# Another cyclic order for the first layer, and the second layer's first buffers loaded while the experts run

## The chip, the cores and the metric

One core of a Trainium2 chip runs one program. Its engines are TensorE (matmuls and transposes), VectorE, ScalarE, GpSimd and SyncE, whose queue issues most DMAs. The metric is the device time of one execution in microseconds. The kernel before takes 4163.48 us, the median of three runs from 4163.27 to 4163.56.

## The reference, cut to what matters

`x` is (64, 128, 256), the context (64, 128, 192), everything float32. Two layers follow each other, each an attention over the context and then a feed-forward part:

```python
x = x + xattn0(layernorm(x), ctx_768, mask)   # 16 heads of 16, masked keys
x = x + moe(layernorm(x))                     # switch router over 8 experts, capacity 512
x = x + xattn1(layernorm(x), ctx_768)         # 16 heads, then relu(out @ W1 + b1) @ W2 + b2
x = x + cells(layernorm(x))                   # 6 nodes, each an 8-head self-attention
```

The router counts, over all tokens in order, how many went to each expert; token 513 and later of an expert keep their input. A cell node forms q, k and v from three edges `We` out of earlier nodes, scaled by `ew`, then applies `Wq`, `Wk`, `Wv`. The kernel multiplies each edge with its projection beforehand ("fusing", pieces F and B), which is eighteen 256 x 256 products.

## The kernel before, in words

Three blocks follow each other; each begins when every engine has ended the one before.

**First layer** (`phase_first_layer`). The 64 sequences are 32 jobs of two. Each engine runs through a written list. A table such as `FIRST_PE_ORDER` is one period; `name:s` means that in period k the piece is done for job k - s (`unfold`). So different jobs are interleaved, and an engine never leaves its list's order. The pieces on TensorE are: `Tx` transposes the normed rows, `Q`, `K`, `V` project, `S0` and `S1` are the scores of either sequence, `T0.0` to `T1.1` transpose the probabilities (two strips each), `A` is attention times V, `O` the output projection, `Tn` transposes the second norm's rows, `L` makes router logits, and `r.n` ranks tokens within experts for each group of four jobs. VectorE takes the strips' maxima (`x`), reciprocals (`i`), copies out of PSUM (names with `^`), statistics (`st`, `st1`) and the routing steps `r.sh`, `r.oh`. ScalarE does the exponentials (`e`) and the copies of transposed probabilities (`T..^`). GpSimd scales the probabilities (`n`), norms rows (`rs`, `nm`, `rs1`, `nm1`) and scatters routed rows with indirect DMAs (`put`).

SyncE's list is written out (`load`, `store`). The context buffer `ct` has two halves. `load(j)` (L282) fetches x and then the context:

```python
                if j >= 2:
                    sp.wait_ge(prod, max(n_prod["K", j - 2], n_prod["V", j - 2]))
                sp.dma_start(ct[:, j % 2], halves(ctx[j])).then_inc(c_in[j % 2], 16)
```

and `K` and `V` of job j wait for `c_in`. `store(j)` (L291) waits for `x1_made` and for `nm1` of job j. The last lines of SyncE's list are stores 29 and 30, then the loads for fusing pieces 3, 4 and 5 (each waits for `B` three before, L280 and L279), then store 31. `FUSE_PE_PLACES` and `FUSE_DVE_PLACES` say behind which piece of which job (counted from the last) a fusing piece is inserted.

**Experts** (`phase_experts`). Eight experts in turn, each 512 rows: transpose, 256 to 1024 with relu, 1024 to 256. SyncE loads rows, w1 and w2 of expert e when expert e - 2 has freed its buffer, and unfused cell weights.

**Second layer** (`phase_second_layer`). Again 32 jobs and one table per engine. `f.` pieces are the cross attention, S, T, A, Q, K, V, O with a digit are a cell node, `e.` the end. Twelve fusing pieces (F6 to F17) are inserted into the first periods; their four buffers lie in `probs` and `probsT`. `f.ga` on GpSimd gathers expert outputs into `routed` with an indirect DMA, `f.x2` on VectorE adds them to x, `f.st`, `f.rs` and `f.x` norm the result, `f.Tx` transposes it. At the end `e.f1` and `e.f2` on GpSimd form the single buffer `fin`, and `e.f1(j)` waits for the store of job j - 1. SyncE's loop is:

```python
            for j in range(2, JOBS):
                load_rows(j)      # waits for f.Tx(j-1)
                load_context(j)   # waits for f.K and f.V of j-1
                if j >= JOBS_IN_FLIGHT:
                    store(j - JOBS_IN_FLIGHT)
```

with `JOBS_IN_FLIGHT` 3; `store` waits for `fin_made`.

Of the kernel before, what the change touches and what calls it, by code (L numbers as in the profile page):

```python
# [139 lines left out]
def phase_first_layer(nc, io, scratch, keep, cst, consts_in, cell, w1_first):  # L140
# [794 lines left out]
def phase_second_layer(nc, io, scratch, keep, cell, cst, out):  # L935
# [52 lines left out]
    def rows(ap, j):  # L988
        return ap.rearrange("(g b) t d -> g t b d", b=PAIR)[j]

    with ExitStack() as es:
# [6 lines left out]
        wq, wk, wv = (sb(n, [2, D]) for n in ("wq", "wk", "wv"))
        w1, w2 = sb("w1", [2, HID * P]), sb("w2", [HID, D])
        bq, bk, bv, b1 = sb("bq", [2]), sb("bk", [2]), sb("bv", [2]), sb("b1", [HID])  # L1000
        b2, ln_g, ln_b = sb("b2", [D]), sb("ln_g", [D]), sb("ln_b", [D])
        x2, x3 = sb("x2", [JOBS_IN_FLIGHT, PAIR, D]), sb("x3", [JOBS_IN_FLIGHT, PAIR, D])
        xg, xn, x5, fin = sb("routed", [PAIR, D]), sb("xn", [PAIR, D]), sb("x5", [PAIR, D]), sb("fin", [PAIR, D])
        ct, xT, qF, kE, kO = (sb(n, [2, W2]) for n in ("ctxT", "xT", "front_qT", "front_kT_even", "front_kT_odd"))
        oF = xT
# [12 lines left out]
        late = [(t[:, 2 * h].rearrange("p j t -> p (j t)").rearrange("p (c n) -> p c n", n=D),  # L1018
                 t[:, 2 * h + 1].rearrange("p j t -> p (j t)").rearrange("p (c n) -> p c n", n=D))
                for t in (pr[:, 1], pT[:, 1]) for h in range(2)]  # L1020
# [40 lines left out]
        def halves(a):  # L1061
            return a.rearrange("(c p) n -> p c n", p=P)

        def late_load(eng, n):
            c, k, edge = fused[n]
            weT, we = late[n % LATE_RING]
            eng.dma_start(weT, halves(io["edgesT"][edge])).then_inc(late_in[n % LATE_RING], 16)
            eng.dma_start(we, halves(io[("L1_ffn_Wq", "L1_ffn_Wk", "L1_ffn_Wv")[k]][c])).then_inc(late_in[n % LATE_RING], 16)
# [4 lines left out]
        def _(sp):  # L1073
            def store(j):
                sp.wait_ge(fin_made, j + 1)
                sp.dma_start(rows(out, j), fin[:]).then_inc(stored[j % 2], 16)
# [8 lines left out]

            def load_context(j):
                if j >= 1:
                    sp.wait_ge(prod, max(n_prod["f.K", j - 1], n_prod["f.V", j - 1]))
                sp.dma_start(ct[:], halves(ctx[j])).then_inc(c_in[j % 2], 16)

            def fuse_load(n):
                sp.wait_ge(prod, n_prod[f"B{n - LATE_RING}", 0])
                late_load(sp, n)
# [490 lines left out]
```

## Time and profile before

| | us |
|---|---|
| median of the runs | 4163.48 |
| the profiled execution | 4160.97 |
| its span, first to last instruction | 4159.2 |
| TensorE busy in the span | 4031.4 (97%) |
| ScalarE busy | 2628.5 (63%) |
| VectorE busy | 2472.9 (59%) |
| GpSimd busy | 1932.9 (46%) |
| mean granted TensorE clock | 0.99 |

The first layer fills the first 653 us or so, the experts 657 to 896, the second layer the rest. In rows of the timeline the first number is the start in us, the second the duration, then engine, line and operation, what it writes and reads, how many instructions are merged, and in brackets how long the engine sat idle just before and what ended that. L12 is line 12 of the kernel. A landing time counts from the issue of a DMA to its completion.

### The profile page before, as it was taken

The page shows a single profiled execution, that of the slowest core. Times are in us where ns is not written, and L with a number is a line of the kernel's source. Part 1 is how long each engine was busy: PE and PEld are TensorE (multiplying, and loading weights), DVE is VectorE, ACT ScalarE, POOL GpSimd, SP SyncE. Part 2 cuts the span into 40 slices and gives each one's busy share as a digit, 9 for nine tenths or more (in the row PEclk, how much of TensorE's full clock was granted, in tenths as well). Part 3 has the DMA queues.
Part 4 walks back from the last instruction along what each step waited for, and adds up shares of the span by engine and source line. Part 5 has one row for each costly group of instructions (what it writes and reads, how often), then busy time and mean ns, then how long its engine had stood idle before and what let it go on. Part 6 is the DMA issues. An engine that isn't in the chain of part 4 may idle for free.

```text
span 4159.2 us, 100757 instructions
## 1 busy us (share of the span) xinstructions
PE 4031.4 (97%) x38276; PEld 3405.7 (82%) x38276; DVE 2472.9 (59%) x6184; ACT 2628.5 (63%) x11786; POOL 1932.9 (46%) x2011
## 2 busy tenths in 40 slices
PE   7999998988999999999999999999999999999997
PEld 6888876666888888888888888888888888888885
DVE  5777772024566666666666666666666666666553
ACT  6888871214666666666666666666666666666664
POOL 6888982113444444444444444444444444444332
PEclk9999999999999999999999999999999999999999
DMA  3232214430000000000000000000000000000000
GB/s 102 70 98 72 70 45 140 132 116 23 12 14 14 14 17 21 13 14 14 13 13 16 13 13 13 12 12 12 12 12 12 12 20 12 12 12 12 7 4 6
DMA packets 117867, 129.75 MB, mean 31 GB/s; under 512 B 12006, under 2 KB 110676, under 8 KB 117264
## 3 DMA queue, kind: packets, MB, share of 16 engines
q1 hardware_dynamic: 101664, 106.26, 8.0%
q0 software_dynamic: 6144, 8.43, 0.7%
q10 hardware_dynamic: 9584, 8.61, 0.7%
q8 instruction: 312, 5.11, 0.5%
q14 instruction: 163, 1.34, 0.1%
HBM read 89.68 MB, written 41.94 MB: 32 GB/s over the span
## 4 chain that ended last, share of the span: by engine, by line
PE 75%; DVE 1%; ACT 1%; DMA 0%; POOL 0%; issue 0%; ACTq 0%; POOLq 0%; SPq 0%; DVEq 0%
PE c_product L1374 35%; PE c_product L1385 15%; PE c_product L1433 10%; PE c_scores L1423 7%; PE c_product L1456 5%; PE c_product L1444 2%; ACT c_probs L1187 1%; DVE c_qT L1233 1%; PE c_product L1362 1%; PE c_product L1493 0%; DVE c_neg_max L1242 0%; DMA c_probsT<-in_L_ffn_Wk 0%; ACT c_front_probs L1187 0%; POOL c_probs L1135 0%; DMA c_probsT<-in_L_ffn_Wv 0%
## 5 line engine op out<-in xcount | busy, mean ns | idle before, releaser
L1135 POOL TENSOR_TENSOR c_probs<-c_probs,c_row_inv 128x512 f32<-128x512 f32 x768 | 794.2, 1044 | 1525.8 <-DVE c_row_inv L1245 1525.1
L1187 ACT ACTIVATE c_probs<-c_scores,c_neg_max 128x128 f32<-128x128 f32 x3072 | 1086.6, 409 | 606.1 <-DVE c_neg_max L1242 606.1
L1374 PE MATMUL c_product<-c_nodes,cell_w 128*128 128x256 f32 x4352 | 1064.2, 384 | 6.1 <-DVE c_nodes L1233 3.9
L1374 PEld LDWEIGHTS c_product<-c_nodes,cell_w 128*128 128x128 f32 x4352 | 802.6, 190 | 133.1 <-DVE c_nodes L1233 12.8
L1187 ACT ACTIVATION_READ_ACCUMULATOR c_probs<-c_scores,c_neg_max 128x1 f32 x3072 | 762.1, 248 | 0.0
L1242 DVE TENSOR_REDUCE c_neg_max<-c_scores 128x4 f32<-128x512 f32 x1024 | 635.6, 683 | 179.7 <-PE c_scores L1423 179.5
L1193 ACT COPY c_probsT<-c_product 128x512 f32<-128x512 f32 x768 | 416.2, 611 | 237.8 <-PE c_product L1433 235.0
L1187 ACT ACTIVATE c_front_probs<-c_scores,c_neg_max 128x128 f32<-128x128 f32 x1024 | 359.0, 401 | 149.0 <-DVE c_neg_max L1242 149.0
L1385 PE MATMUL c_product<-cell_w,c_nodes 128*128 128x256 f32 x1792 | 432.7, 381 | 1.6 <-DVE c_kT L1233 1.6
L1433 PE MATMUL c_product<-consts_sb,c_probs 128*128 128x128 f32 x3072 | 403.1, 275 | 15.2 <-POOL c_probs L1135 15.0
L420 ACT ACTIVATE a_probs<-a_scores,a_neg_max 128x128 f32<-128x128 f32 x1024 | 361.9, 399 | 82.3 <-DVE a_neg_max L476 81.7
L1433 PEld LDWEIGHTS c_product<-consts_sb,c_probs 128*128 128x128 f32 x3072 | 349.7, 141 | 59.5 <-POOL c_probs L1135 21.2
L1385 PEld LDWEIGHTS c_product<-cell_w,c_nodes 128*128 128x128 f32 x1792 | 332.8, 190 | 47.7 <-DVE c_kT L1233 1.9
L1135 POOL TENSOR_TENSOR c_front_probs<-c_front_probs,c_row_inv 128x512 f32<-128x512 f32 x256 | 266.7, 1057 | 179.7 <-DVE c_row_inv L1245 179.6
L1374 PE MATMUL c_product<-c_oT,cell_w 128*128 128x256 f32 x1280 | 328.7, 379 | 1.3 <-DVE c_oT L1233 1.3
L1245 DVE RECIPROCAL c_row_inv<-c_row_sum 128x4 f32<-128x4 f32 x1024 | 171.7, 168 | 183.8 <-ACT c_probs L1187 140.8
L1233 DVE TENSOR_SCALAR c_nodes<-c_product,cell_b 128x256 f32<-128x256 f32 x320 | 140.0, 479 | 236.8 <-PE c_product L1374 236.8
L1233 DVE TENSOR_SCALAR c_qT<-c_product,cell_b 128x256 f32<-128x256 f32 x384 | 167.8, 478 | 180.6 <-PE c_product L1374 180.6
L1374 PEld LDWEIGHTS c_product<-c_oT,cell_w 128*128 128x128 f32 x1280 | 243.0, 190 | 35.0 <-DVE c_oT L1233 2.0
L369 POOL TENSOR_TENSOR a_probs<-a_probs,a_row_inv 128x512 f32<-128x512 f32 x256 | 259.3, 1047 | 26.6 <-DVE a_row_inv L479 26.6
L1233 DVE TENSOR_SCALAR c_oT<-c_product,cell_b 128x256 f32<-128x256 f32 x384 | 168.1, 479 | 159.3 <-PE c_product L1456 156.8
L1187 ACT ACTIVATION_READ_ACCUMULATOR c_front_probs<-c_scores,c_neg_max 128x1 f32 x1024 | 246.3, 240 | 0.0
(167 smaller groups left out, 6679.4 us busy)
## 6 DMA issues: line engine op xcount, KB each, us to landing
e_w<-in_L_ffn_w SPq DMA_DIRECT2D x12, 1024.0 KB, 6.5
a_x<-in_x SPq DMA_DIRECT2D x32, 256.0 KB, 2.9
a_ctxT<-in_ctx_pairsT SPq DMA_DIRECT2D x32, 256.0 KB, 3.1
x<-a_x SPq DMA_DIRECT2D x32, 256.0 KB, 2.2
xn<-a_xn SPq DMA_DIRECT2D x32, 256.0 KB, 2.1
c_routed<-xn SPq DMA_DIRECT2D x32, 256.0 KB, 2.9
c_x<-x SPq DMA_DIRECT2D x32, 256.0 KB, 3.2
c_ctxT<-in_ctx_pairsT SPq DMA_DIRECT2D x32, 256.0 KB, 2.8
```

Of the source, the lines that this page charges most:

```text
L369: nc.gpsimd.tensor_tensor(p, p, rinv[:, j % 2, b, r].unsqueeze(2).broadcast_to([P, 4, T]), ALU.mult).then_inc(norm_made, 1)
L420: a = nc.scalar.activation(pr[:, j % 2, b, r, k], S[r][:, k], ACT.Exp, bias=nmax[:, j % 2, b, r, k:k + 1], accum_out=rsum[:, j % 2, b, r, ...
L1135: nc.gpsimd.tensor_tensor(e, e, rinv[:, i, r].unsqueeze(2).broadcast_to([P, 4, T]), ALU.mult).then_inc(norm_made, 1)
L1187: a = nc.scalar.activation(probs(n)[:, r, k], S[r][:, k], ACT.Exp, bias=nmax[:, i, r, k:k + 1], accum_out=rsum[:, i, r, k:k + 1])
L1193: nc.scalar.copy(probsT(n)[:, int(n[-1])], bank(n, j)[:]).then_inc(pT_made, 1)
L1233: k = V.tensor_scalar(dst[:, u], m[:, u], bias[:, u:u + 1], scalar, ALU.add, *([then] if then else []))
L1242: V.tensor_reduce(nmax[:, i, r], S[r][:], AX.X, ALU.max, negate=True).then_inc(max_made, 1)
L1374: i = T_.matmul(m[:, u], w[:, k, u * P:(u + 1) * P], src[:, k], start=n == 0, stop=n == last)
L1385: i = T_.matmul(m[:, b], src[:, k, b * T:(b + 1) * T], w[:, k], start=n == 0, stop=n == len(steps) - 1)
L1423: i = T_.matmul(S[r][:, k], q[e, u, b * T:(b + 1) * T], w[e, u, b * T:(b + 1) * T], start=True, stop=True)
L1433: i = T_.transpose(m[:, k], probs(name)[:, r, k], ident)
L1456: i = T_.matmul(m[32 * r:32 * r + 32, u, b * T:(b + 1) * T], va[:, group(c), b, h:h + 32], pT[:, group(c), r, k], start=True, stop=True)
```

## The change

The tables of the first layer are replaced, and with them the places of its fusing pieces; the ring of `xn1` has seven places instead of six. The second layer's weights, biases, the buffers of its first four fusing pieces and the rows, x and context of its job 0 are allocated before the experts and loaded by SyncE in their loop; the engines' own loads at the start of the second layer are gone. The first expert's w1 now lies in `front_probs`. The first w2 waits for the first rows. In the second layer, `front_oT` gets a buffer of its own, two memsets move behind the first gather, and the store moves.

```diff
 FIRST_PE_ORDER = """
-K:1 T0.1:3 S1:2 Tx:1 A:3 r.n:6 Q:1 O:3 T1.0:2 T0.0:2 S0:1 V:1 L:5 Tn:4 T1.1:2
+S1:2 A:3 Tx:1 Tn:6 O:3 r.n:7 Q:1 T0.0:2 S0:1 V:2 T0.1:2 K:0 L:6 T1.0:2 T1.1:2
 FIRST_DVE_ORDER = """
-r.oh:5 S0.i0:1 K^:0 S0.i1:1 S1.x0:1 Tx^:0 S1.x1:1 S1.x3:1 S1.i0:1 A^:2 r.n^:5 S1.x2:1 S1.i1:1 Q^:0 S1.i3:1
-O^:2 S0.i3:1 S1.i2:1 st1:2 S0.i2:1 S0.x0:0 S0.x1:0 S0.x3:0 V^:0 L^:4 r.sh:4 mk:-1 st:-1 S0.x2:0 Tn^:3
+r.oh:6 S1.x3:1 S0.i2:1 S1.x2:1 A^:2 S1.x1:1 Tx^:0 S1.x0:1 Tn^:5 r.n^:6 S1.i3:1 O^:2 Q^:0 S1.i1:1 S1.i0:1
+S1.i2:1 S0.x1:0 S0.x3:0 S0.x0:0 S0.x2:0 V^:1 mk:-1 st:-1 K^:-1 L^:5 r.sh:5 st1:2 S0.i1:0 S0.i3:0 S0.i0:0
 FIRST_ACT_ORDER = """
-S1.e1:1 S1.e3:1 S1.e2:1 T1^0:1 T1^1:1 T0^0:1 T0^1:1 S0.e0:0 S0.e1:0 S0.e3:0 r.ex:4 T1^2:1 S0.e2:0 T1^3:1
-T0^3:1 T0^2:1 S1.e0:0
+T1^0:5 T1^3:5 T1^2:5 S1.e3:4 S1.e2:4 S1.e1:4 S1.e0:4 T0^0:4 T0^1:4 S0.e1:3 S0.e0:3 T0^2:4 T0^3:4 S0.e3:3
+S0.e2:3 r.ex:8 T1^1:4
 FIRST_POOL_ORDER = """
-rs:1 nm:1 rs1:4 S0.n0:2 nm1:4 S0.n1:2 S1.n0:2 S1.n1:2 S1.n3:2 S1.n2:2 S0.n3:2 S0.n2:2 put:9
+S0.n1:3 S0.n2:3 nm1:5 S1.n3:3 S1.n1:3 S1.n0:3 S1.n2:3 put:11 rs:1 nm:1 rs1:4 S0.n3:2 S0.n0:2
 FUSE_PE_PLACES = """
-Tn:1 F0
-L:1 B0
-Tn:0 F1
-L:0 B1 F2 F3
-r.n:0 B2 B3 F4 F5 B4 B5
+L:5 F0
+T1.0:1 B0 F1
+Tn:4 B1
+L:4 F2
+T1.0:0 B2 F3
+T1.1:0 B3 F4
+Tn:3 B4
+L:3 F5
+Tn:2 B5
...
-    X_RING, ROW_RING, GROUP = 4, 6, 4
+    X_RING, ROW_RING, GROUP = 4, 7, 4
... phase_experts, SyncE
+            sp.wait_ge(rows_in[0], 16)
             sp.dma_start(w2t[:, 0], tiles(w2[0])).then_inc(w2_in[0], 16)
...
+                if e == 4:
+                    for n, a in (("wk", "L1_xattn_Wk_rows"), ("wq", "L1_xattn_Wq"), ("wv", "L1_xattn_Wv_rows"),
+                                 ("w1", "L1_xattn_W1"), ("w2", "L1_xattn_W2")):
+                        sp.dma_start(early[n][:], tiles(io[a])).then_inc(early[n + "_in"], 16)
+                if e == 5:
+                    for n in ("bq", "bk", "bv", "b1"):
+                        sp.dma_start(early[n][:], io[f"L1_xattn_{n}_cols"]).then_inc(early["column_biases_in"], 16)
+                    for n, a in (("b2", "L1_xattn_b2"), ("ln_g", "L1_ffn_ln_g"), ("ln_b", "L1_ffn_ln_b")):
+                        sp.dma_start(early[n][:], io[a].partition_broadcast(P)).then_inc(early["row_biases_in"], 16)
+                if e == 6:
+                    for n in range(FUSED_FIRST, FUSED_FIRST + len(early["late"])):
+                        fuse_load(sp, io, fused, n, early)
+                if e == E - 1:
+                    sp.dma_start(early["routed"][:], rows_of(scratch["xn1"], 0)).then_inc(early["rows0_in"], 16)
+                    sp.dma_start(early["x"][:, 0], rows_of(scratch["x1"], 0)).then_inc(early["x0_in"], 16)
+                    sp.dma_start(early["ctxT"][:], tiles(io["ctx_pairsT"][0])).then_inc(early["ctx0_in"], 16)
... phase_second_layer, SyncE
-FRONT_NODES, JOBS_IN_FLIGHT = 2, 3
+FRONT_NODES, JOBS_IN_FLIGHT, STORES_BEHIND = 2, 3, 5
...
             for j in range(2, JOBS):
                 load_rows(j)
+                if j >= STORES_BEHIND:
+                    store(j - STORES_BEHIND)
                 load_context(j)
-                if j >= JOBS_IN_FLIGHT:
-                    store(j - JOBS_IN_FLIGHT)
-            for j in range(JOBS - JOBS_IN_FLIGHT, JOBS):
+            for j in range(JOBS - STORES_BEHIND, JOBS):
                 store(j)
```

`phase_first_layer`'s SyncE list and its context buffer are not edited.

## Rows read from the trace of the kernel before

**Rows 1.** Busy time by stage; columns are window, length, then each engine's us
```profile
100.00:600.00 500.00, 479.42 (x5845) 413.61 (x5844) 382.24 (x1064) 417.28 (x1941) 444.62 (x478) 0.99 0.23 72
660.00:896.00 236.00, 230.99 (x832) 154.06 (x832) 21.46 (x32) 43.98 (x64) 21.19 (x19) 0.98 0.36 120
1200.00:4000.00 2800.00, 2797.34 (x26917) 2401.20 (x26917) 1750.03 (x4260) 1855.71 (x8369) 1214.36 (x1246) 1.00 0.04 13
```
**Rows 2.** Timeline of VectorE, the copy of oT, one per job, eight jobs apart
```profile
122.79 0.69 DVE L501 COPY a_oT<-a_product 128x512 f32<-128x512 f32 x1
270.99 0.69 DVE L501 COPY a_oT<-a_product 128x512 f32<-128x512 f32 x1
```
**Rows 3.** Windows of 10 us with idle of TensorE; the clock stands third from the end
```profile
150.00:160.00 10.00, 7.43 (x111) 6.29 (x114) 9.28 (x33) 6.67 (x32) 6.63 (x9) 1.00 0.00 1
...
300.00:310.00 10.00, 7.32 (x112) 6.20 (x114) 9.16 (x32) 6.57 (x32) 8.33 (x10) 0.87 0.07 23
...
530.00:540.00 10.00, 8.22 (x89) 7.13 (x90) 7.82 (x25) 5.81 (x32) 7.71 (x9) 0.83 0.24 79
```
**Rows 4.** Timeline near the start: V of job 1, a turn, the context load
```profile
41.12 1.99 PE L618 MATMUL a_product<-a_wv,a_ctxT 128*128 128x256 f32 x8
42.95 1.04 PE L651 MATMUL a_product<-consts_sb,a_probs 128*128 128x128 f32 x8
43.15 0.37 SPq L289 DMA_DIRECT2D a_ctxT<-in_ctx_pairsT  x1
```
**Rows 5.** Landing times in us: of L289 in the first layer, and second layer medians
```profile
DMA to landing us min/median/max: 2.5/3.1/8.3
...
out<-c_fin SPq DMA_DIRECT2D x28, 256.0 KB, 2.2
...
c_ctxT<-in_ctx_pairsT SPq DMA_DIRECT2D x27, 256.0 KB, 2.8
c_routed<-y,slots POOLq DMA_INDIRECT x54, 2.7
```
**Rows 6.** Timeline of TensorE, a turn and the K behind it
```profile
150.61 1.04 PE L651 MATMUL a_product<-consts_sb,a_probs 128*128 128x128 f32 x8
151.49 1.89 PE L611 MATMUL a_product<-a_ctxT,a_wk 128*128 128x256 f32 x8
```
**Rows 7.** Timeline of the first layer's tail, each engine
```profile
595.17 0.39 PE L632 MATMUL a_scores<-a_mask_add,a_one_row 32*128 32x512 bf16 x4
...
619.47 1.94 PE L662 MATMUL a_product<-a_probsT,a_v_even_odd 128*32 128x128 f32 x60 [0.82 <-ACT a_probsT L426]
...
621.04 2.43 POOL L355 TENSOR_SCALAR a_xn<-a_x,a_mean_var,a_rstd 128x256 f32<-128x256 f32 x2 [0.30 <-DMA buf<-a_xn,slots]
...
649.85 0.98 POOL L396 DMA_INDIRECT buf<-a_xn,slots  x1 [0.30 <-issue]
...
657.74 0.36 SPq L761 DMA_DIRECT2D e_rows<-buf  x1
```
**Rows 8.** Timeline of the second layer's start
```profile
896.97 0.37 SPq L1081 DMA_DIRECT2D c_routed<-xn  x1
...
903.95 3.78 PE L1374 MATMUL c_product<-c_probsT 128*128 128x256 f32 x8 [10.35 <-DMA c_probsT<-in_L_ffn_Wq]
...
908.86 1.99 PE L1374 MATMUL c_product<-c_probsT 128*128 128x256 f32 x8
...
918.55 0.60 PE L1362 MATMUL c_product<-consts_sb,c_routed 128*128 128x128 f32 x4
```
**Rows 9.** Timeline of one period of the second layer
```profile
2047.03 1.28 POOL L1162 TENSOR_TENSOR c_fin<-c_x,c_ln_g 128x512 f32<-128x512 f32 x1 [0.23 <-DVE c_x L1227]
...
2048.17 0.60 PE L1362 MATMUL c_product<-consts_sb,c_routed 128*128 128x128 f32 x4
...
2053.31 1.08 POOL L1141 DMA_INDIRECT c_routed<-y,slots  x1 [1.70 <-DMA c_routed<-xn]
...
2059.38 1.63 DVE L1252 SCALAR_TENSOR_TENSOR c_x<-c_routed,gates,c_x 128x256 f32<-128x256 f32 x2
...
2063.91 1.04 PE L1433 MATMUL c_product<-consts_sb,c_probs 128*128 128x128 f32 x8
```

More of the change, by code:

```diff
@@ L55, with rows_of, half_rows, fuse_load @@
 TO_Q, TO_K, TO_V, EDGE, OUT = range(KINDS)
+def rows_of(ap, j):
+    return ap.rearrange("(g b) t d -> g t b d", b=PAIR)[j]
+def half_rows(a):
+    return a.rearrange("(c p) n -> p c n", p=P)
+def fuse_load(eng, io, fused, n, early):
+    c, k, edge = fused[n]
+    r = n % len(early["late"])
+    weT, we = early["late"][r]
+    eng.dma_start(weT, half_rows(io["edgesT"][edge])).then_inc(early["late_in"][r], 16)
+    eng.dma_start(we, half_rows(io[("L1_ffn_Wq", "L1_ffn_Wk", "L1_ffn_Wv")[k]][c])).then_inc(early["late_in"][r], 16)
 def cell_plan():
@@ L729, in phase_experts @@
     plan = cell_plan()
+    fused = fused_weights(plan)
     with ExitStack() as es:
@@ L932, with phase_second_layer @@
 """
-def phase_second_layer(nc, io, scratch, keep, cell, cst, out):
+def phase_second_layer(nc, io, scratch, keep, cell, cst, early, out):
     ctx = io["ctx_pairsT"]
@@ L996, in sem @@
             return es.enter_context(nc.semaphore("c_" + name))
[L998 to L1005, printed above, removed]
+        wq, wk, wv, w1, w2 = (early[n] for n in ("wq", "wk", "wv", "w1", "w2"))
+        bq, bk, bv, b1, b2, ln_g, ln_b = (early[n] for n in ("bq", "bk", "bv", "b1", "b2", "ln_g", "ln_b"))
+        xg, x2, ct, pr, pT, prF = (early[n] for n in ("routed", "x", "ctxT", "probs", "probsT", "front_probs"))
+        x3 = sb("x3", [JOBS_IN_FLIGHT, PAIR, D])
+        xn, x5, fin = sb("xn", [PAIR, D]), sb("x5", [PAIR, D]), sb("fin", [PAIR, D])
+        xT, qF, kE, kO = (sb(n, [2, W2]) for n in ("xT", "front_qT", "front_kT_even", "front_kT_odd"))
+        oF = sb("front_oT", [2, W2])
         vE, vO = sb("v_even", [PAIR, D]), sb("v_odd", [PAIR, D])
@@ L1059, in bank, with loaded @@
             return M[bank_of[n, j] % BANKS]
[L1061 to L1068, printed above, removed]
+        def loaded(eng, pair, first, j):
+            eng.wait_ge(*((first, 16) if j == 0 else (pair[j % len(pair)], 16 * ((j - 1) // len(pair) + 1))))
         block = es.enter_context(nc.Block())
@@ L1075, in store, with next_fuse_load @@
                 sp.wait_ge(fin_made, j + 1)
-                sp.dma_start(rows(out, j), fin[:]).then_inc(stored[j % 2], 16)
+                sp.dma_start(rows_of(out, j), fin[:]).then_inc(stored[j % 2], 16)
             def load_rows(j):
-                if j >= 1:
-                    sp.wait_ge(prod, n_prod["f.Tx", j - 1])
-                sp.dma_start(xg[:], rows(scratch["xn1"], j)).then_inc(r_in[j % 2], 16)
+                sp.wait_ge(prod, n_prod["f.Tx", j - 1])
+                sp.dma_start(xg[:], rows_of(scratch["xn1"], j)).then_inc(r_in[j % 2], 16)
                 if j >= JOBS_IN_FLIGHT:
                     sp.wait_ge(x3_done, j - JOBS_IN_FLIGHT + 1)
-                sp.dma_start(x2[:, j % JOBS_IN_FLIGHT], rows(scratch["x1"], j)).then_inc(x_in[j % JOBS_IN_FLIGHT], 16)
+                sp.dma_start(x2[:, j % JOBS_IN_FLIGHT], rows_of(scratch["x1"], j)).then_inc(x_in[j % JOBS_IN_FLIGHT], 16)
             def load_context(j):
[L1087 to L1093, printed above, removed]
-            load_rows(0)
-            load_context(0)
-            for t, a, got in ((wk, "L1_xattn_Wk_rows", wk_in), (wq, "L1_xattn_Wq", wq_in), (wv, "L1_xattn_Wv_rows", wv_in)):
-                sp.dma_start(t[:], halves(io[a])).then_inc(got, 16)
-            fuse_load(FUSED_FIRST + LATE_RING)
+                sp.wait_ge(prod, max(n_prod["f.K", j - 1], n_prod["f.V", j - 1]))
+                sp.dma_start(ct[:], half_rows(ctx[j])).then_inc(c_in[j % 2], 16)
+            def next_fuse_load(n):
+                sp.wait_ge(prod, n_prod[f"B{n - len(late)}", 0])
+                fuse_load(sp, io, fused, n, early)
+            later = list(range(FUSED_FIRST + len(late), len(fused)))
+            next_fuse_load(later[0])
             load_rows(1)
-            for n in range(FUSED_FIRST + LATE_RING + 1, len(fused)):
-                fuse_load(n)
+            for n in later[1:]:
+                next_fuse_load(n)
             load_context(1)
@@ L1137, in _ @@
                 elif n == "f.ga":
-                    pool.wait_ge(r_in[j % 2], 16 * (j // 2 + 1))
+                    loaded(pool, r_in, early["rows0_in"], j)
                     for b in range(PAIR):
```

81 lines of the change are left out of this document (42 added, 39 removed).

## The prediction

> **What bounds the kernel now.** I read the stage windows first. In the first layer (100 to 600 us) TensorE is busy 479.42 of 500 us, GpSimd 444.62 and ScalarE 417.28; in the second layer (1200 to 4000) TensorE is busy 2797.34 of 2800 [rows 1]. So the second layer has nothing to give on TensorE and can only lose, the first layer has 4.1% of idle, and the rest lies at the seams: 600 to 660, and the start of the second layer.
>
> Then the rhythm of the first layer, from VectorE's copies of `oT`, one per job: eight jobs take 270.99 - 122.79 = 148.2 us, 18.53 each [rows 2]. With 95.9% busy that is 17.77 us of TensorE work per job and 0.76 of idle. The idle sits in the job of each group of four that carries the routing: 7.43 of 10 us busy at 150, 7.32 at 300, the last at 530 [rows 3].
>
> Then the DMA queue: which event lets a context load go, and how long it takes to land [rows 4, 5]. This decides the case.
>
> **The change part by part.**
>
> *First layer, context loads (the largest term).* `ct` has two halves. SyncE may issue the load for job j only when K(j-2) and V(j-2) are done, and K(j) on TensorE waits for it. The old table has V:1 and K:1: V(j-2) is in period j-1 and K(j) in period j+1, with more than a period between. The new table reads `V:2 T0.1:2 K:0`: unfolded, V(j-2), T0.1(j-2), K(j). Only one turn stands between the instruction that frees the buffer and the one that needs it full. The ring and the wait are not edited. In the trace V(1) starts at 41.12 and ends at 43.11, and SyncE issues the context load at 43.15 [rows 4]. That transfer lands in 2.5 at least and 3.1 at the median, behind another load; the same transfer of the second layer, which leaves alone as this one now will, takes 2.8 [rows 5]. So K could start at 43.15 + 2.8 + 0.1 = 46.05. TensorE would be ready earlier: the turn begins at 42.95 [rows 4] and holds it 151.49 - 150.61 = 0.88 [rows 6], to 43.83. The wait is 2.2 us (1.9 with 2.5, 2.5 with 3.1). TensorE issues in order, and behind K(j) stand L, T1.0, T1.1, S1, A and the rest of its period, so nothing fills it. The period becomes 17.77 + 2.2 = 19.97 if every other wait goes, 1.44 more than now. The first jobs sit in the fill, where TensorE is idle for other reasons; 28 jobs remain: 28 x 1.44 = **+40** (32 to 49). The gain that the new order brings, 0.76 per job or 21 us in all, is already taken in full here.
>
> *The clock after such waits.* The granted clock fell in some of the old idle stretches and not in others: 1.00 at 150 to 160, 0.87 at 300 to 310, 0.83 at 530 to 540 [rows 3]; of six such stretches three fell. One fall costs 0.13 to 0.17 of 10 us. New waits are of similar length but in one piece. I take one in four: 7 x 1.5 = **+10**; ends 0 and, if all fall, 28 x 1.5 = 42.
>
> *First layer, tail.* Old: from S0(31) at 595.17 the last A ends at 619.47 + 1.94 = 621.41 (26.2 later), the last scatter is issued at 649.85, and the experts' first load leaves at 657.74 [rows 7]. New: F3 and F4 stand before A(31). But F3's weights are loaded by SyncE behind store(30), which waits for nm1(30): GpSimd ended that at 621.04 + 2.43 = 623.47, 28.3 after S0(31) [rows 7]. Two stores' and loads' issue (0.9) and a landing of 3.1 [rows 5] put F3 at 32.3. TensorE's own work from S0(31) to F3 is about 25 (seven projections of 1.83, six turns of 0.88, and small pieces, by the strides in [rows 4, 6]), so it waits some 7 us; with F3, T1.1, B3, F4 and A another 7, A(31) ends near 39.5, 13.3 later than now. V(30) and one turn, 2.7 us, have moved behind S0(31), which leaves 10.6. Behind A(31) the chain O, `nm1`, Tn, L, routing, scatter is unchanged, but the fusing pieces no longer hold up its TensorE steps; I give 3 back: **+8** (from -3, if that chain turns out shorter by all that the pieces took, to +12).
>
> *Experts.* Twenty-three small loads go into SyncE's stream. Each expert's loads are issued an expert or more ahead of their use and TensorE is busy 230.99 of 236 us [rows 1]; they are hidden, 0. Holding the first w2 back until the rows are in may bring 0.5 at the start: **-0.5** (-1 to +1). If the cover is gone, one late weight load costs its landing, some 3 us [rows 5].
>
> *Start of the second layer.* Old: its first issue is at 896.97, TensorE starts F6 at 903.95 after 10.35 of idle for the fused weights, F7 waits again until 908.86, and f.Tx starts at 918.55 [rows 8]. New: all four buffers are there. F7 to F10 with their pieces take 918.55 - 908.86 = 9.7, F6 and B6 2.6 more: f.Tx at 896.97 + 12.3 = 909.3, 9.2 earlier. GpSimd's gather can leave at 896.97 and its landing, statistics and normalising fit in those 12 us. What is late next is F11's load, issued only after f.Tx as before, so all behind it shifts as a block: **-9** (-6 to -11; low clock at the start may keep 2).
>
> *Second layer, the store's place.* Store(j-5) is now issued in iteration j, just behind load_rows(j), which waits for f.Tx(j-1). e.f1(j-4) of that same period needs that store landed, since `fin` is one buffer. Old: e.f1 ran at 2047.03, before f.Tx (2048.17) had even ended [rows 9]. New: f.Tx ends at 2048.77, two loads are issued, the store leaves near 2049.7 and lands 2.2 later alone [rows 5], up to 1 more behind the loads: e.f1 starts near 2052.7, 5.7 late. Behind it on GpSimd stand e.f2, S3.n0 and the gather. The gather used to wait for its rows until 2053.31 [rows 9]; now it starts near 2056.4, its second half near 2057.8, and lands 2.7 later [rows 5], at 2060.5 to 2061.2. VectorE's f.x2 started at 2059.38 [rows 9], so it is 1.1 to 1.9 late, and behind it O0^ ends near 2063.7. TensorE needs O0^'s bank for T3.1, which began at 2063.91 [rows 9]. So the whole delay just fits: 27 periods at 0.1, **+2** (0 to 27 x 0.7 = 19). Nothing is gained by the move, TensorE being full.
>
> *Own buffer for `front_oT`, memsets behind the gather, seven rings for xn1*: off the path, 0 (-1 to +1).
>
> Sum: 40 + 10 + 8 - 0.5 - 9 + 2 = +50.5 on the profiled execution's 4160.97, whose span is 4159.2. The runs' median is 2.5 higher: about **4213**.
>
> **The rivals.**
> 1. *The clock falls at every context wait.* For: half the old stretches fell, with no longer idle. Against: the other half didn't. 4213 - 10 + 42 = 4245. The Trainium skill ("TensorE: Matmul & The Clock Gate", section "HAM oscillation") tells of a kernel that alternates short bursts with DMA waits and drops to the low clock in every one; the trace only half agrees.
> 2. *The store in the second layer bites.* If the store lands a microsecond later than I think, T3.1 waits 0.6 in 27 periods: 4213 + 14 = 4227.
> 3. *Faster: the context is not late.* It decides if K(j) finds its context landed, by a load issued earlier than V(j-2)'s end. Then the period is 17.8: 28 x -0.7 = -20, tail +8, start -9, second layer +2: 4144. Against it stand the rows of the issue, 0.04 after V's end.
> 4. *The wait is smaller*: landing 2.5, no clock loss, a tail no worse than before: 32 - 9 + 2 puts it near 4189.
>
> **How the numbers follow.** Forecast 0.60 (its own range 4195 to 4235), rival 1 0.17, rival 2 0.10, rival 3 0.06, rival 4 0.07. The range 4185 to 4250 takes in all but rival 3 and the ends. A measurement tells 0.2% (8 us) from no change; faster is rival 3 alone, 0.06; the same 0.02; slower 0.92.
>
> **What would show it.** TensorE idle about 2.2 us before each L611 matmul that reads `ctxT`, put down to the DMA of `ctxT`, about thirty times; `oT` copies 20 us apart, all alike; a wait of several us before an `edge_w` matmul near the end of the layer; F6 within a microsecond of the block's start; GpSimd's `c_fin` waiting for the DMA of `out`. No wait on `ctxT`, or a period under 18.5, would refute me.

## The result, and the profile after

The changed kernel takes 4309.71 us (median of 4 runs, 4300.49 to 4322.68) beside 4163.52 for the kernel before (4163.27 to 4163.81): ratio 1.0355, 95% interval [1.0342, 1.0368]. It is slower, as forecast, but by 146 us and not by 50. The profiled execution of after has a span of 4311.1 us and a mean clock of 0.975.

Split at marks that both traces have ([rows 7, 8] for before), the spans differ like this:

| stretch | before | after | more | forecast |
|---|---|---|---|---|
| start to the mask matmul of S0(31) | 595.17 | 688.97 | +93.8 | +47 (40 + 10, less the 2.7 moved behind) |
| S0(31) to the end of A(31) | 26.24 | 41.90 | +15.7 | +13.3 |
| A(31) to the experts' first load | 36.33 | 38.81 | +2.5 | -3 |
| that load to f.Tx of job 0 | 260.81 | 254.65 | -6.2 | -9.5 |
| f.Tx to the end | 3240.65 | 3286.77 | +46.1 | +2 |

Windows of after, in the columns of [rows 1]: window, length, each engine's us, then clock, DMA share and GB/s.

```profile
100.00:600.00 500.00, 434.48 (x4944) 379.12 (x4943) 325.66 (x906) 356.89 (x1660) 376.76 (x403) 0.92 0.21 64
...
1300.00:4100.00 2800.00, 2761.77 (x26442) 2363.98 (x26441) 1766.87 (x4194) 1823.43 (x8234) 1188.27 (x1228) 1.00 0.04 13
```

In the first layer TensorE is idle for 65 of 500 us where it was idle for 21, and the clock is 0.92 where it was 0.99 [rows 1]: two losses, idle and slow work. In the second layer the window reads a clock of 1.00 as before, and 38 us of 2800 are idle, where 2.7 were. The waits of TensorE in the first layer (total, times, longest):

```profile
PE a_product L636 <- DMA a_ctxT<-in_ctx_pairsT: 63.8, 30, 2.9
PE a_product L643 <- DVE a_oT L526: 21.3, 9, 3.9
```

The first row is the predicted wait: 30 times 2.1 us. The second was not foreseen. The rhythm shows the whole effect on the steady part. VectorE's copies of `oT` for jobs 4 and 28, first in before (its job 4 is the first row of [rows 2]), then in after:

```profile
571.66 0.69 DVE L501 COPY a_oT<-a_product 128x512 f32<-128x512 f32 x1
```

```profile
133.35 0.69 DVE L526 COPY a_oT<-a_product 128x512 f32<-128x512 f32 x1 [0.44 <-PE a_product L687]
...
664.42 0.69 DVE L526 COPY a_oT<-a_product 128x512 f32<-128x512 f32 x1 [0.44 <-PE a_product L687]
```

Over these 24 jobs one takes 18.70 us in before and 22.13 in after: 3.43 more, where the prediction had 1.44 more and a period of 19.97. TensorE's timeline around both waits (start, duration, instruction; in brackets the idle before it and what ended it):

```profile
200.60 3.59 PE L643 MATMUL a_product<-a_wo,a_oT 128*128 128x256 f32 x8 [3.74 <-DVE a_oT L526]
...
213.34 3.06 PE L636 MATMUL a_product<-a_ctxT,a_wk 128*128 128x256 f32 x8 [2.03 <-DMA a_ctxT<-in_ctx_pairsT]
216.19 1.72 PE L643 MATMUL a_product<-a_wsw,a_xn1T 128*128 128x8 f32 x8
217.75 3.49 PE L676 MATMUL a_product<-consts_sb,a_probs 128*128 128x128 f32 x16
...
235.78 1.99 PE L636 MATMUL a_product<-a_ctxT,a_wk 128*128 128x256 f32 x8 [2.01 <-DMA a_ctxT<-in_ctx_pairsT]
237.61 0.95 PE L643 MATMUL a_product<-a_wsw,a_xn1T 128*128 128x8 f32 x8
238.42 2.01 PE L676 MATMUL a_product<-consts_sb,a_probs 128*128 128x128 f32 x16
...
255.72 3.78 PE L636 MATMUL a_product<-a_ctxT,a_wk 128*128 128x256 f32 x8 [2.76 <-DMA a_ctxT<-in_ctx_pairsT]
```

Read the durations: K takes 1.99 us behind one wait and 3.06 or 3.78 behind another; the same L takes 0.95 or 1.72, the same pair of turns 2.01 or 3.49. After some waits the engine runs its next matmuls at the lower of its two levels (1.2 GHz), after others of the same length it doesn't. By windows of 10 us the granted clock is 0.71 at 210, 0.75 at 250 and 0.78 at 560, and 1.00 at 160. The Trainium skill ("TensorE: Matmul & The Clock Gate", section "HAM oscillation") has the clock fall in every DMA wait of a loop whose bursts of 2 us alternate with waits of 3 to 5 us. The waits here are shorter and lie about 20 us apart, and only a part of them is followed by the low clock: the trace agrees in part.

The tail of after, SyncE's and TensorE's rows; they answer to [rows 7]:

```profile
716.83 0.36 SPq L322 DMA_DIRECT2D xn<-a_xn  x1
717.24 0.47 SPq L304 DMA_DIRECT2D a_edgeT<-in_edgesT  x1
717.75 0.51 SPq L305 DMA_DIRECT2D a_edge_w<-in_L_ffn_Wq  x1
...
769.68 0.36 SPq L787 DMA_DIRECT2D e_rows<-buf  x1
```

```profile
688.97 0.39 PE L657 MATMUL a_scores<-a_mask_add,a_one_row 32*128 32x512 bf16 x4
...
720.99 3.78 PE L636 MATMUL a_product<-a_edge_w,a_edgeT 128*128 128x256 f32 x8 [6.87 <-DMA a_edge_w<-in_L_ffn_Wq]
...
728.92 1.95 PE L687 MATMUL a_product<-a_probsT,a_v_even_odd 128*32 128x128 f32 x64
```

F3 waits 6.87 us for weights that SyncE issues right behind store(30): as forecast (7). F3 begins 32.0 after S0(31) (forecast 32.3), A(31) ends 41.9 after it (39.5).

The start of the second layer, against [rows 8]:

```profile
1008.71 3.06 PE L1390 MATMUL c_product<-c_probsT 128*128 128x256 f32 x8 [3.42 <-PEq L757]
...
1013.12 3.51 PE L1390 MATMUL c_product<-c_probsT 128*128 128x256 f32 x8
...
1017.28 1.97 PE L1390 MATMUL c_product<-c_probs 128*128 128x256 f32 x8
...
1024.33 0.60 PE L1378 MATMUL c_product<-consts_sb,c_routed 128*128 128x128 f32 x4
```

The 10.35 us of idle are gone. F6 and F7 take 3.06 and 3.51 us where F8 takes 1.97, after 3.42 us of idle at the block's border, so about 3 of the 9 us are lost again to slow work: 6 stay.

The second layer's waits, all engines and TensorE's (columns as above); before had no such row on `c_fin` for a DMA:

```profile
POOL c_fin L1186 <- DMA out<-c_fin: 179.3, 27, 8.5
DVE c_x L1264 <- DMA c_routed<-y,slots: 47.3, 27, 3.8
PE c_product L1449 <- DVE c_nodes L1245: 33.6, 27, 2.3
```

One period of it, to be laid on [rows 9], whose f.Tx began at 2048.17 (here 2174.18):

```profile
2174.18 0.60 PE L1378 MATMUL c_product<-consts_sb,c_routed 128*128 128x128 f32 x4
...
2175.73 0.47 SPq L1104 DMA_DIRECT2D out<-c_fin  x1
...
2179.03 1.27 POOL L1186 TENSOR_TENSOR c_fin<-c_x,c_ln_g 128x512 f32<-128x512 f32 x1 [6.21 <-DMA out<-c_fin]
...
2182.80 1.08 POOL L1162 DMA_INDIRECT c_routed<-y,slots  x1 [0.17 <-issue]
...
2185.24 3.03 POOL L1156 TENSOR_TENSOR c_probs<-c_probs,c_row_inv 128x512 f32<-128x512 f32 x3
...
2187.03 2.92 DVE L1264 SCALAR_TENSOR_TENSOR c_x<-c_routed,gates,c_x 128x256 f32<-128x256 f32 x2 [1.55 <-DMA c_routed<-y,slots]
...
2191.01 1.06 PE L1449 MATMUL c_product<-consts_sb,c_probs 128*128 128x128 f32 x8 [0.92 <-DVE c_nodes L1245]
```

Counted from f.Tx: e.f1 at 4.85 (forecast 4.5), the gather at 8.6 (8.2), f.x2 at 12.9 (before 11.2, forecast 12.3 to 13.1). So far all as worked out. Then f.x2 takes 2.92 us, not 1.63, and T3.1 begins at 16.8 where it began at 15.7: 1.1 us late in this period, not 0.1. The step has come to lie beside four products of GpSimd on end, the three above and

```profile
2188.23 1.03 POOL L1156 TENSOR_TENSOR c_front_probs<-c_front_probs,c_row_inv 128x512 f32<-128x512 f32 x1
```

where in before one of 1.19 us lay beside it. The 27 periods from job 4 on, in before and in after, columns as above:

```profile
1261.24:3917.13 2655.89, 2653.33 (x25490) 2277.96 (x25489) 1665.15 (x4051) 1759.95 (x7939) 1157.30 (x1189) 1.00 0.05 13
```

```profile
1368.91:4069.64 2700.73, 2662.60 (x25491) 2278.71 (x25489) 1707.64 (x4051) 1757.95 (x7939) 1150.42 (x1189) 1.00 0.04 13
...
1368.91:1472.35 103.44, 100.37 (x946) 85.65 (x945) 63.19 (x151) 65.29 (x295) 42.56 (x44) 0.98 0.05 14
```

These 27 periods hold 44.8 of the 46.1 us: 35.6 of idle and 9.3 of longer work. Every period of before takes 98.4 us, those of after 99.4 to 103.5, and the two longest are the only ones with a clock of 0.98.

### The profile page after: what moved, and what is told of

Its sections match the earlier page's. It is cut to its first block, busy times and chain, and to the rows that moved or that the text cites. A ratio compares the mean times of both kernels' runs of the same rounds, so it can differ in the third digit from the quotient of the medians.

```text
span 4311.1 us, 100757 instructions
## 1 busy us (share of the span) xinstructions
PE 4075.8 (95%) x38276; PEld 3443.6 (80%) x38276; DVE 2512.5 (58%) x6184; ACT 2626.7 (61%) x11786; POOL 1928.0 (45%) x2011
## 4 chain that ended last, share of the span: by engine, by line
PE 63%; DVE 4%; DMA 4%; POOL 3%; ACT 1%; issue 1%; SPq 1%; POOLq 0%; DVEq 0%
PE c_product L1390 28%; PE c_product L1401 13%; PE c_product L1449 10%; PE c_scores L1439 6%; PE c_product L1472 4%; DMA out<-c_fin 2%; DVE c_x L1264 2%; DMA c_routed<-y,slots 2%; PE c_product L1460 1%; ACT c_probs L1202 1%; POOL c_fin L1186 1%; POOL c_fin L1190 1%; DVE c_qT L1245 1%; POOL c_probs L1156 1%; PE c_product L1378 1%
## 5 line engine op out<-in xcount | busy, mean ns | idle before, releaser
L1449 PE MATMUL c_product<-consts_sb,c_probs 128*128 128x128 f32 x3072 | 406.2, 276 | 50.9 <-DVE c_nodes L1245 33.6
L445 ACT ACTIVATION_READ_ACCUMULATOR a_probs<-a_scores,a_neg_max 128x1 f32 x1024 | 253.3, 247 | 0.0
```

The costliest lines, as they stand in the source:

```text
L445: a = nc.scalar.activation(pr[:, j % 2, b, r, k], S[r][:, k], ACT.Exp, bias=nmax[:, j % 2, b, r, k:k + 1], accum_out=rsum[:, j % 2, b, r, ...
L1449: i = T_.transpose(m[:, k], probs(name)[:, r, k], ident)
```

## The experiments

The experiments ran on several chips; the kernel before lay at 4163.3 to 4163.9 on each of them.

**The first layer's order undone (e1_old_tables).** On the changed kernel; the other three orders and both tables of the fused products go back in the same way:

```diff
-S1:2 A:3 Tx:1 Tn:6 O:3 r.n:7 Q:1 T0.0:2 S0:1 V:2 T0.1:2 K:0 L:6 T1.0:2 T1.1:2
+K:1 T0.1:3 S1:2 Tx:1 A:3 r.n:6 Q:1 O:3 T1.0:2 T0.0:2 S0:1 V:1 L:5 Tn:4 T1.1:2
...
-    X_RING, ROW_RING, GROUP = 4, 7, 4
+    X_RING, ROW_RING, GROUP = 4, 6, 4
```

> The changed kernel with the first layer's four tables, the fusing places and the ring of six as before; all else changed. In the traces the experts' first load leaves at 769.68 instead of 657.74, 112 us later, and from f.Tx to the end it takes 3286.8 instead of 3240.7, 46 longer, while the second layer's start gained 6. Theory (each cost belongs to its own edit): the first layer's 112 go and the second layer's stay: 4310 - 112 = 4198. Rival (the second layer's loss is only the wake of the first layer's, as by my forecast of +2 for the store): some 4157.

4205.23 us, ratio 1.0100 [1.0083, 1.0116]. The theory said 4198 and its rival 4157: the rival is out. The new order costs 104.5 us; 42 of the loss lie elsewhere.

**A third context buffer (e2_ctx_ring3).**

```diff
-        ct = sb("ctxT", [2, 2, W2])
+        ct = sb("ctxT", [3, 2, W2])
-                if j >= 2:
-                    sp.wait_ge(prod, max(n_prod["K", j - 2], n_prod["V", j - 2]))
+                if j >= 3:
+                    sp.wait_ge(prod, max(n_prod["K", j - 3], n_prod["V", j - 3]))
... c_in and the places that read ct likewise by j % 3
```

> The changed kernel with three context buffers in the first layer instead of two, so that the load for job j waits for K and V of job j-3. Theory: the 30 waits of K on the context (63.8 us in the trace) go, and most of the low clock behind them (mean 0.92 over 100 to 600): 64 + 25 = 90 less, 4220, jobs 18.6 apart. Rival 1 (the low clock comes from other idle stretches, as the ones by the routing): only the 64 go, 4246. Rival 2 (another wait takes the place, ScalarE or VectorE bounding the period): less than 30 gained, above 4280.

4230.38 us, ratio 1.0168: 79.3 less than the changed kernel. TensorE's waits for the context fall from 63.8 us (30 times) to 8.3 (11), and the clock is 0.98 over 100 to 600. Two rows on TensorE stay, and one on GpSimd:

```profile
PE a_product L643 <- DVE a_oT L526: 24.8, 10, 3.9
PE a_product L636 <- DMA a_ctxT<-in_ctx_pairsT: 8.3, 11, 1.4
...
PE a_product L636 <- DMA a_edge_w<-in_L_ffn_Wq: 7.0, 1, 7.0
```

```profile
652.99 1.10 POOL L421 DMA_INDIRECT buf<-a_xn,slots  x1 [21.47 <-DVE slots L591]
```

The rhythm of this kernel, jobs 4 and 28 again:

```profile
120.80 0.69 DVE L526 COPY a_oT<-a_product 128x512 f32<-128x512 f32 x1 [0.44 <-PE a_product L687]
...
581.12 0.69 DVE L526 COPY a_oT<-a_product 128x512 f32<-128x512 f32 x1 [0.49 <-PE a_product L687]
```

That is 19.18 us per job, 2.95 less than in after and still 0.48 more than before. This is what my sum had missed: I had assumed that the new order removed the 0.76 us of idle per job. With its contexts in time it makes the steady part longer, not shorter. The wait stands in the routing jobs, as it did before. In before it was for K's copy (six times, 1.8 us each), here it is for `oT` (six times in the window 100 to 620 us, 22.5 us). In before:

```profile
PE a_product L662 <- DVE a_kT_odd L494: 10.7, 6, 1.8
```

In both kernels r.oh stands on VectorE in front of the copy: eight chained instructions and eight additions. In e2 its first instruction, its fifth, the additions and the copy of `oT` behind it are

```profile
170.40 0.19 DVE L569 TENSOR_REDUCE a_mx<-a_exp 128x8 f32<-128x64 f32 x1
...
171.38 1.07 DVE L573 TENSOR_TENSOR a_one_hot<-a_gate_probs,a_pm 128x64 f32<-128x64 f32 x1
...
174.48 1.57 DVE L578 TENSOR_TENSOR a_tokens_before<-a_tokens_before,a_one_hot 128x8 f32<-128x8 f32 x8
...
177.23 0.68 DVE L526 COPY a_oT<-a_product 128x512 f32<-128x512 f32 x1
```

The chain takes 5.65 us here and 3.71 in before. The difference lies in three of its instructions on two SBUF operands, L573, L574 and L576, which take 1.07, 0.96 and 0.71 us where in before (L548, L549 and L551) they take 0.22 to 0.28. First GpSimd's row beside them in e2, then L573's counterpart in before:

```profile
171.32 3.05 POOL L394 TENSOR_TENSOR a_probs<-a_probs,a_row_inv 128x512 f32<-128x512 f32 x3
```

```profile
154.79 0.22 DVE L548 TENSOR_TENSOR a_one_hot<-a_gate_probs,a_pm 128x64 f32<-128x64 f32 x1
```

In before GpSimd runs no such product there but its scaling of `a_xn` (2.47 us from 153.88). The chain is 1.94 us longer and the wait grew from 1.8 to 3.75, so the two agree. No run moved GpSimd's products away, so this part is read from the traces and not tested.

**The store one job nearer (e3_store4).**

```diff
-FRONT_NODES, JOBS_IN_FLIGHT, STORES_BEHIND = 2, 3, 5
+FRONT_NODES, JOBS_IN_FLIGHT, STORES_BEHIND = 2, 3, 4
```

> The changed kernel with STORES_BEHIND 4 instead of 5 in the second layer: the store of job j-4 is issued in iteration j, a period before e.f1 needs the buffer again. Theory: e.f1's wait for the DMA of out (179 us over 27 periods) goes, the gather leaves earlier, VectorE does not wait for it, and TensorE's wait for O0's bank (33.6 us, 27 times) goes: 37 to 44 less, about 4268. Rival (the second layer is longer for another reason, as front_oT's own buffer or the memsets): 4310, within the scatter of its runs.

4266.16 us, ratio 1.0248: 43.5 less than the changed kernel. The `c_fin` row is gone; the costliest row of GpSimd on `c_fin` is 6.5 us in all. The 27 periods take 98.4 us each again. From the experts' first load to the end the trace takes 3493.2 us and that of after 3541.5: 48.3 less. The first layer of this run ends 2.0 later (771.67 against 769.68), so the two times differ by less than the store costs.

**Work in place of the context wait (e4_filled_wait).** From job 2 on, eight matmuls of `wk` with `wo` go into K's bank ahead of its context wait; K overwrites them.

```diff
+                    if j >= 2:
+                        pe.wait_ge(wo_in, 16)
+                        project(m, wk, wo)
                     pe.wait_ge(c_in[o], 16 * (j // 2 + 1))
```

> The changed kernel with eight additional matmuls on constant weights (wk and wo, 1.8 us at full clock) into K's own bank just before K waits for the context; K writes over them. Nothing else changes, and they lie in 2.0 us of idle. Theory (the waits let the clock fall, which lengthens what comes behind): granted clock in the first layer back to 0.97 or more, 25 to 30 us less, about 4282. Rival (the clock falls elsewhere, and the matmuls delay K by their overhang): 4310 or up to 10 more.

4285.5 us, ratio 1.0291: 24.2 less than the changed kernel though it does more work. K still starts when its context is there; only the idle before it is filled, and its rows fall to 12.2 us in all. The waits for `oT` are no shorter than in after (24.0 and 21.3 us, nine times each). What comes back is the clock:

```profile
100.00:600.00 500.00, 470.05 (x5409) 407.55 (x5407) 341.85 (x950) 376.76 (x1752) 398.00 (x427) 0.98 0.22 67
```

So the 79.3 of the third buffer are 63.8 - 8.3 = 55.5 of wait and 24 of clock. The rhythm says the same: this kernel takes 20.94 us per job between jobs 4 and 28, so of the 3.43 that after takes more than before, 1.19 are clock, 1.76 the wait and 0.48 the order itself. In this profiled run the first layer ends 30.4 sooner than in after and the rest takes longer by 10.7, so 24 may be some us too little for the clock.

**Early loads alone, store four behind (e5_old_store4).** The first experiment's edit and the third's together.

> The changed kernel with the four orders of the first layer, the places of the fused products and the ring of six rows as they were before, and with the store of the finished rows four jobs behind and not five. Only the early loads of the second layer are left of the change. My theory is that the order of the first layer and the store's distance are the whole loss and that they add: the kernel with the old orders alone took 4205.2 us, and four jobs in place of five took 43.5 us off the changed kernel (4309.7 to 4266.2), so 4161.7 us here, within 4157 to 4165, which is 2 us under the kernel before. Rival: the store takes as much back as a third of it even at four jobs, because it still stands third in line behind the two row loads where before it came after the context; then some 4175 us, over the kernel before. Second rival: the early loads give their whole 7 to 9 us once nothing else is in the way, 4155 us.

4155.95 us (11 runs), ratio 0.9981 [0.9972, 0.9990]: 0.2% faster than the kernel before. From the experts' first load (659.95) to the first product on the front's oT (950.82, in before 955.18) it takes 290.9 us where before took 297.4, and from there to the end both take 3204.0: the early loads bring 6.6 us and the store, four behind, costs nothing. Beyond that the first layer ends 1 to 2 us later in the traces with its old orders (658.97 and 659.95 against 657.74), which I haven't explained. The result lies at the second rival's 4155, below the theory's 4157 to 4165. The store's distance gives 48.2 us here (3494.8 from the experts' first load to the end, 3543.0 in e1), as with the new order.

**The tail's loads first (e6_loads_first).** On the kernel with three context buffers:

```diff
-            for j in range(JOBS - X_RING + 1, JOBS - 1):
-                store(j)
             for n in range(RING, FUSED_FIRST):
                 sp.wait_ge(prod, n_prod[f"B{n - RING}", JOBS - 1])
                 fuse_load(n)
+                if n < FUSED_FIRST - 1:
+                    store(JOBS - FUSED_FIRST + n)
```

> The kernel with three context buffers (4230.4 us), and in SyncE's list at the end of the first layer the loads of the fourth and fifth fused product stand ahead of the stores of jobs 29 and 30 and not behind both. Theory of the prediction's tail term: F3's wait of 7.0 us on its edge weights goes, and it was on the path, so the one-hot chain of the last full group on VectorE, the slots, the rows that GpSimd sends and the first expert load all come 7 us sooner: 4223 us, within 4221 to 4226; the wait of GpSimd on the slots falls from 21.5 to some 14 us. Rival: GpSimd's own list bounds the tail and would be late anyway; then the wait goes and the time stays at 4230 within 2.

4224.07 us, ratio 1.0151: 6.3 less. F3's wait is gone, GpSimd's wait for the slots is 11.5 us, and the experts' first load leaves at 680.19 and not at 684.87.

**The one-hot chain later (e7_onehot_later).** On the same base; on VectorE `r.oh:6` moves from the head to behind `Q^:0`, and `r.n^:6` to behind `K^:-1`:

```diff
-S1:2 A:3 Tx:1 Tn:6 O:3 r.n:7 Q:1 T0.0:2 S0:1 V:2 T0.1:2 K:0 L:6 T1.0:2 T1.1:2
+S1:2 A:3 Tx:1 Tn:6 O:3 Q:1 T0.0:2 S0:1 V:2 T0.1:2 K:0 r.n:7 L:6 T1.0:2 T1.1:2
...
```

> The kernel with three context buffers (4230.4 us), with the routing's one-hot chain (L569 to L578, some 5.3 us of VectorE) moved from the head of VectorE's round, where it stands ahead of A^, to behind Q^, and its product r.n moved on TensorE from behind O to behind K. Theory: TensorE's wait of 3.9 us for a_oT at each routing job (10 seen) is made by this chain alone and VectorE has room for it later in the round, so 8 to 10 waits of 3.9 us go and little comes in their place: 4230 - 31..39 plus some 5 for K^ and V^ that come later, 4195 to 4205 us, with the group average of a job falling from 18.5 to some 17.6 us. Rival: VectorE is full in a routing job (13.4 us of its own work in 17.3 and 5.3 more for the chain), so the wait only moves to another product (S0's maxima, K^ or V^) and the time stays within 5 us of 4230.

4248.35 us, ratio 1.0205: 18 more. Both theories fail. The wait for `a_oT` is down to 0.7 us, but not because VectorE had room, as the rows read: the slots come later, GpSimd waits for them in order, and its next rows come late for TensorE.

```profile
POOL buf L421 <- DVE slots L591: 46.6, 8, 24.1
```

```profile
PE a_product L629 <- POOL a_xn L380: 17.4, 7, 5.6
PE a_product L636 <- DMA a_ctxT<-in_ctx_pairsT: 16.6, 15, 2.2
PE a_product L722 <- DVE a_tokens_before L578: 11.7, 3, 4.6
```

**All of them (e8_combined).** Third buffer, store four behind, loads first, chain later.

> Everything that the runs so far point to in one kernel: three context buffers, store four jobs behind, the two loads of fused products ahead of the stores at the tail, the one-hot chain behind Q^. If the terms add: 4230.4 - 43.5 (store) - 7 (tail) - 30 (chain) = 4150 us, under the kernel before (4163.5); with the rival on the chain 4180 us. If the new order of the first layer has a cost of its own that none of these touches, it stays over 4190.

4188.85 us, ratio 1.0062 [1.0049, 1.0076]. It lies over both of my figures (4150 and 4180), because the chain's move costs 18 where I had it bring 30 or nothing: 4230.4 - 43.5 - 6.3 + 18.0 = 4198.6, and the kernel is 10 under that. Its trace says where: the first layer ends 5.8 later than in e2 (690.70 against 684.87), where the chain and the loads alone moved it by +18.7 and -4.7, and what follows takes 44.2 less (3494.6 against 3538.8). So the chain costs less in this company than alone.

**The tail's fused products behind the routing (e9_tail_behind_route).** On e6, the store four behind, and:

```diff
-T1.0:0 B2 F3
-T1.1:0 B3 F4
-Tn:3 B4
-L:3 F5
-Tn:2 B5
+T1.0:0 B2
+r.n:4 F3
+L:3 B3
+Tn:1 F4
+L:1 B4
+L:0 F5
+r.n:0 B5
```

> The kernel with three context buffers and the two loads ahead of the stores (4224.1 us), with the store four jobs behind, and with the fused products F3, F4 and F5 of the first layer's tail moved: on TensorE behind the routing product r.n of the last full group (job 27), behind Tn of job 30 and behind L of job 31, on VectorE their copies likewise behind the slots. The store alone gives 4224.1 - 43.5 = 4180.6. Theory of the tail: what ends the first layer is GpSimd, which waits 11.5 us for the slots of group 27 and then sends 14 rows of 1.28 us each one after another; F3, F4 and their copies stand ahead of that group's one-hot chain and of A^, and take some 5 to 7 us on both engines; with them behind, slots, rows and the first expert load come 5 to 7 us sooner: 4175 us, within 4172 to 4178. It still ends some 15 us behind the old orders there, since the new order makes the slots of a group one round later. Rival: the pieces cost as much behind as ahead (they then stand in front of L and the last one-hot chains): 4181 within 2.

4167.97 us (10 runs), ratio 1.0010 [1.0001, 1.0020]: 12.6 under the 4180.6 that the sum gives, twice what I expected; no run has all but the move. The traces split it: against e6 the experts' first load leaves at 673.79 and not at 680.19, 6.4 sooner, inside the 5 to 7 expected, and what follows takes 48.0 less (3540.8 to 3492.8), which is the store and not the move. GpSimd goes on at 641.53 after 5.56 us of waiting for the slots. The load is still 16 behind [rows 7], and 12.9 of that stand already at the mask matmul of S0(31) (608.08 against 595.17).

**Two buffers for the finished rows (e10_two_fin).** On e1, the store still five behind:

```diff
-        xn, x5, fin = sb("xn", [PAIR, D]), sb("x5", [PAIR, D]), sb("fin", [PAIR, D])
+        xn, x5, fin = sb("xn", [PAIR, D]), sb("x5", [PAIR, D]), sb("fin", [2, PAIR, D])
-                    if j >= 1:
-                        pool.wait_ge(stored[(j - 1) % 2], 16 * ((j - 1) // 2 + 1))
+                    if j >= 2:
+                        pool.wait_ge(stored[j % 2], 16 * (j // 2))
... e.f1, e.f2 and store by fin[:, j % 2]; the front's oT on xT
```

> The kernel with the old orders and the early loads, the store still five jobs behind (4205.2 us), but with two buffers for the finished rows (c_fin), so that GpSimd's product for job j waits for the store of job j-2 and not of job j-1; to make room, the front's oT lies on xT again as before. Theory: the bite of the late store is only GpSimd's wait on c_fin (6 us each period), which makes the gather, x and the whole front late; with two buffers that wait is gone and the time falls to that of four jobs behind, 4156 us, within 4153 to 4160. Rival: the place in the queue itself costs (the store of 256 KB lies third behind the two row loads and lands in 3.3 and not 2.2 us, and slows the loads beside it); then part of the 44 us stays, 4170 to 4205.

4156.04 us (10 runs), ratio 0.9982 [0.9972, 0.9992], to 0.1 us the time of four jobs behind. The store still goes out third in line and lands in

```profile
out<-c_fin SPq DMA_DIRECT2D x32, 256.0 KB, 3.3
```

so neither its place nor its landing costs anything; the one buffer did. (The front's `oT` has its own buffer in e5 and lies on `xT` here, and the two take the same time.)

## Why the prediction was wrong

The direction and the first mechanism were right, and the time lay 97 us over the forecast and 60 over my range. The steps that failed are the second and the sixth, and the third was sized too small. Step by step:

1. *"The wait is 2.2 us", 28 times.* 2.1 us, 30 times, and the third buffer took most of them away (8.3 us stay). Right.
2. *"The gain that the new order brings, 0.76 per job or 21 us in all, is already taken in full here."* This failed. I wrote "if every other wait goes" and didn't test it against the diff. The new VectorE order begins with `r.oh:6` and has `A^:2` behind it, as the old one had `K^:0` behind `r.oh:5`. [rows 3] show VectorE at 9.2 to 9.3 of 10 us in two routing jobs, and those are windows of the old idle, too. With the contexts in time (e2) a job takes 19.18 us where it took 18.70: not 0.76 less but 0.48 more, 1.24 per job or some 35 us off over 28 jobs. The chain's wait did not go, it doubled (10.7 to 22.5 us). My 18.53 per job was itself taken over eight jobs; over 24 it is 18.70.
3. *The clock, "+10 (one in four)".* Mis-sized. Filling the waits gave back 24.2 us (30 in the first layer of the trace), which by the 1.5 us per fall that I used is about one wait in two (by the trace's 30, two in three), the share of [rows 3] that I had before me and marked down. Rival 1, all 28 of them for 42, was too much.
4. *The tail, +8.* F3 and A(31) came within 0.3 and 2.4 us of the forecast. What failed is *"the fusing pieces no longer hold up its TensorE steps; I give 3 back"*: the stretch behind A(31) grew by 2.5. Its end is GpSimd, which waits 21 us for the slots of group 27 and then sends 14 rows at 1.28 us each; those slots are made a round later than before, and behind F3 and F4. By the traces, loads first and products behind gave 4.7 and 6.4 back, more than the whole +8.
5. *Second layer's start, -9.* -6, with F6 and F7 at the low clock. The text had named this ("may keep 2"); it kept 3.
6. *The store, "+2", "the whole delay just fits".* This failed. The largest surprise of a single line: 43.5 us by the times with the new order, 49.2 with the old one (4205.2 to 4156.0), and 48 by the traces with either. Rival 2 named the place and gave it 0.10 and 14 us. My chain of times held up to the start of f.x2. I then took that step at the 1.63 us which it had in [rows 9], with one product of GpSimd beside it; beside four of them on end it took 2.92. A margin of 0.1 us, after four estimated steps, should have been priced as a coin toss between 0 and 27 us, not as +2. The TensorE row on `c_nodes` names 33.6 of the 46.1 us. The others lie in the same 27 periods and not at the layer's ends: 2 more of idle and 9.3 of longer work, of which 4 are in the two periods at the lower clock. Why just those two fell isn't shown.

Added up, the parts give 104.5 for the first layer's order and 49.2 for the store, less 7.9 for the rest with the early loads: 145.8 of the 146.2 us. Such a chain of differences closes by itself and proves nothing; that these two parts add is shown by the store's 48 us under either order. Rival 3 (the context not late) was refuted by the first trace row. The range was too narrow because I let errors stand singly at their middle; the tail and the store lay over the upper ends that I had given them, and the idle gain had no range at all. (The sum itself, 4160.97 + 50.5 + 2.5, is 4214 and not 4213, which changes nothing.)

Could the new order win at all? With a third buffer, the tail mended and the store nearer it stands at 4167.97, where the old order with the same early loads stands at 4156. Its steady part is longer than the old one, 19.2 us per job against 18.7, which is 13 of the 16 us that its first layer ends late; the tail has the other 3. The version to keep is e5 or e10.

## What to carry to other kernels

Before an order searched with measured durations is trusted, list for each ring buffer the instruction that frees it and the one that needs it full, and see that a landing time fits between them; a search that knows durations and not landings will put them side by side. When a single buffer lies between a producer and a store, a store moved later turns into the producer's wait: give it a second buffer or keep the store near. And when a delay "just fits", or an order is searched with measured durations, ask what each VectorE instruction on two SBUF operands will now run beside.

## What the runs showed that I had not expected

- The VectorE instruction on two SBUF operands, `c_x<-c_routed,gates,c_x`, has no fixed duration. In after 29 of its 64 executions touch no work of GpSimd and take 0.47 to 0.48 us. The other 35 take up to 3.16, and their duration is the time for which GpSimd works beside them plus some 0.2 us (median). The longer one of each pair takes 1.26 in most periods of before, 2.4 to 3.2 in those of after with the late store, and at most 1.27 again with the store four behind. The Trainium skill ("GPSIMD Engine Reference", section "1. Specifications") says that the two engines share their SBUF interfaces and contend for instructions with two SBUF inputs; these rows agree. The same shows in the first layer's one-hot chain (0.22 to 1.07 us for one and the same instruction), so both steps that failed failed on durations taken from a place where GpSimd was doing something else. No run tests that by itself.
- Useless matmuls in a wait of 2 us made the kernel 24 us faster (4309.7 to 4285.5).
- The same 256 KB store lands in 2.2 us (median) where it is issued by itself after the context load, and in 3.3 us right behind two row loads. As soon as nothing waits for it, that costs nothing.
